# Attention step loop: biases as 128x32 matmuls beside the products, and a new order of the matmuls of a step

## The reference

```
proj = x @ w_in.T                     # k, v, q, 16 heads of 8 columns
bias[h, i, j] = f_h(i - j)            # a sum of 16 Gaussians of the distance
logits = q @ k.T / sqrt(8) + bias
out = softmax(logits) @ v
```

## Time and profile before

| | |
|---|---|
| median of three runs | 1123.06 us (1118.01 to 1123.2) |
| span of the profiled execution | 1119.0 us (its time outside the span is not shown) |
| granted TensorE clock, mean over the span | 0.931 |
| PE busy | 975.8 us, 87% of the span |
| DVE busy | 853.2 us, 76% |
| ACT busy | 677.5 us, 61% |
| POOL busy | 487.5 us, 44% |
| attention's step loop | about 70 to 503 us |

### The profile page before, as it was taken

The page is one execution under the profiler, slowest core; times in us unless marked ns, Lnnn a source line. Parts: engine busy times, 40 slices in busy tenths (PEclk is TensorE's granted clock), DMA queues, the critical chain, the costliest instruction groups (busy, mean ns, idle before and its releaser), DMA issues. The chain is left out here.

```text
span 1119.0 us, 17095 instructions
## 1 busy us (share of the span) xinstructions
PE 975.8 (87%) x5565; PEld 543.6 (49%) x5565; DVE 853.2 (76%) x2203; ACT 677.5 (61%) x1042; POOL 487.5 (44%) x454
## 2 busy tenths in 40 slices
PE   4889999999999999994999999972777449999998
PEld 2413232223222322323777888731566337778886
DVE  7688888889888988766798555477897787975543
ACT  4226656565656565562668888768334126788886
POOL 4400101101110110101788999814674027889997
PEclk9559999999999999996999999987899659999999
DMA  4930224131313230003466677300000035676973
GB/s 100 281 107 9 79 71 85 35 101 55 71 34 104 53 70 2 1 2 87 143 177 175 160 198 191 96 20 1 0 0 0 3 93 151 172 179 158 218 197 96
DMA packets 80086, 105.65 MB, mean 94 GB/s; under 512 B 17741, under 2 KB 41091, under 8 KB 80003
## 3 DMA queue, kind: packets, MB, share of 16 engines
q1 hardware_dynamic: 78119, 102.42, 35.7%
q10 hardware_dynamic: 1883, 2.21, 0.7%
HBM read 95.84 MB, written 8.52 MB: 93 GB/s over the span
## 5 line engine op out<-in xcount | busy, mean ns | idle before, releaser
L663 POOL TENSOR_TENSOR f_act_low<-f_act,f_act_high 128x512 fp32r<-128x512 f32 x272 | 353.0, 1315 | 151.2 <-ACT f_act_high L639 143.5
L1506 DVE CUSTOM_DVE_ANT_0 at_rows<-at_rows,at_table_max 128x512 f32<-128x512 f32 x512 | 340.0, 718 | 43.6 <-PE at_rows L1292 42.9
L1452 ACT ACTIVATE at_prob<-at_cols 128x1024 f32<-128x1024 f32 x256 | 248.2, 1021 | 185.8 <-PE at_cols L1326 185.8
L678 DVE SCALAR_TENSOR_TENSOR f_gated<-f_hid,f_cw 128x512 f32<-128x512 f32 x256 | 174.0, 687 | 115.1 <-ACT f_act L644 86.9
L644 ACT ACTIVATE f_act<-f_gated 128x512 f32<-128x512 f32 x272 | 171.7, 631 | 110.2 <-DVE f_gated L678 78.5
L639 ACT CAST f_act_high<-f_act 128x512 fp32r<-128x512 f32 x272 | 164.7, 606 | 0.0
L1326 PE MATMUL at_cols<-at_table_cols,flip_sum 128*64 128x512 f16 x1024 | 139.3, 389 | 0.0
L1338 PE MATMUL at_pv<-at_prob,at_v_stack 128*32 128x512 f32 x1024 | 137.2, 608 | 0.2 <-ACT at_prob L1452 0.2
L1292 PE MATMUL at_rows<-at_k_stack,at_q_stack 48*128 48x512 bf16 x512 | 122.5, 408 | 12.8 <-DVE at_maxima L1506 10.1
L610 PE MATMUL f_acc<-f_act_high,wd_high 128*128 128x512 f32 x272 | 109.4, 402 | 9.0 <-POOL f_act_low L663 8.8
L1292 PEld LDWEIGHTS at_rows<-at_k_stack,at_q_stack 48*128 48x128 bf16 x512 | 28.9, 93 | 170.2 <-DVE at_maxima L1506 116.8
(11 more groups left out here) (322 smaller groups left out, 1351.0 us busy)
## 6 DMA issues: line engine op xcount, KB each, us to landing
f_cw<-f_c_rows SPq DMA_DIRECT2D x256, 256.0 KB, 4.5
at_table_cols<-bias_rows SPq DMA_DIRECT2D x32, 248.0 KB, 5.1
at_table_max<-bias_rows SPq DMA_DIRECT2D x12, 480.0 KB, 4.6
at_q_stack<-q_parts SPq DMA_DIRECT2D x32, 96.0 KB, 2.5
at_k_stack<-k_parts SPq DMA_DIRECT2D x24, 96.0 KB, 3.8
at_raw_weights<-in_L_ffn_up_w_dram SPq DMA_DIRECT2D x8, 256.0 KB, 4.3
at_raw_weights<-in_L_ffn_down_w_dram SPq DMA_DIRECT2D x8, 256.0 KB, 4.9
at_table_max<-bias_rows ACTq DMA_DIRECT2D x4, 480.0 KB, 8.0
```

Of the source, the lines that this page charges most:

```text
L663: nc.gpsimd.tensor_tensor(act_l[:, n % PART_SLOTS, :], act[:, n % ACT_SLOTS, :], act_h[:, n % PART_SLOTS, :].bitcast(F32), ALU.subtract).t ...
L678: ins = nc.vector.scalar_tensor_tensor(out=gated[:, n % GATE_SLOTS, :], in0=hid[:, n % HID_SLOTS, :], scalar=0.0, in1=cw[:, k % C_SLOTS, u ...
L1452: act(prob[:, S % 2, 2 * hp:2 * hp + 2, :], s2[:, hp, :, :], ACT.Exp).then_inc(exp_done, 1)
L1506: nc.vector.tensor_tensor_reduce(out=slot, in0=slot, in1=t_max[:, 2 * p.hp + j, c:c + BANK][:, ::-1], scale=1.0, scalar=-3.0e38, op0=ALU.a ...
```

## The change

Biases are made with sixteen matmuls of 32 output columns instead of eight of 64 in a step, each with half the columns of `flip_sum`, on four column strips as the products have them. And all steps have one order: first pair, scores 0, turned maxima (where there are any), second pair, scores 1, the wait for the bias table (where a chunk of it is new), biases 0 and 1, products of the step before. The slots, their order, DVE's, ACT's, POOL's and SP's programs stay as they are.

```diff
                 def biases(S, hp):
                     for j in range(2):
-                        for u in range(2):
-                            c = step_columns(S % STEPS, u)
-                            last = mm(s2[u * HALF:(u + 1) * HALF, hp, j, :], m.flip_sum[:],
+                        for w in range(4):
+                            c, k0 = step_columns(S % STEPS, w // 2), 32 * (w % 2)
+                            last = mm(s2[32 * w:32 * (w + 1), hp, j, :], m.flip_sum[:, k0:k0 + 32],
                                       t_col[:, 2 * hp + j, c:c + BANK], start=False, stop=True)
                     last.then_inc(cols_ready, 1)
...
-                    if pairs:
-                        for hp in range(2):
-                            scores(S, hp)
-                        if phase_turned_in(S) is not None:
-                            turn_maxima(phase_turned_in(S))
-                        if it % BATCH == 0:
-                            for c in range(CHUNKS):
-                                if chunk_starts[c] == s:
-                                    pe.wait_ge(tab_in[c], 32 * (it // BATCH + 1))
-                        for hp in range(2):
-                            biases(S, hp)
-                        for n in pairs[1:]:
-                            rows_pair(n)
-                    else:
-                        for hp in range(2):
-                            scores(S, hp)
-                            biases(S, hp)
-                            if hp == 0 and phase_turned_in(S) is not None:
-                                turn_maxima(phase_turned_in(S))
+                    scores(S, 0)
+                    if phase_turned_in(S) is not None:
+                        turn_maxima(phase_turned_in(S))
+                    for n in pairs[1:]:
+                        rows_pair(n)
+                    scores(S, 1)
+                    if it % BATCH == 0:
+                        for c in range(CHUNKS):
+                            if chunk_starts[c] == s:
+                                pe.wait_ge(tab_in[c], 32 * (it // BATCH + 1))
+                    for hp in range(2):
+                        biases(S, hp)
                     if S > 0:
                         products(S - 1)
```

## The result

After: 1195.92 us (median of four runs, 1192.46 to 1200.12) against 1121.36 for before in the same comparison. The ratio is 1.0694, 95% interval 1.066 to 1.0728: 75 us slower, 1202 was forecast, with a range of 1170 to 1220.

The account below looks back on a forecast made before the run. PE was taken to bound the ordinary step at 3.06 us, with ACT's and DVE's loops close; 74 + 2 + 1 + 2 = +79 on the median 1123.06 gave 1202 us, range 1170 to 1220.

Parts of the forecast that it names:

- The second rows pair waits until 1.23 after the first rows matmul: Ordinary step: PE waits for DVE to free the first of three slots; step 3.66 us against 3.06, +0.60.
- DVE idle about 1 us ahead of each step: Sign the forecast is right: DVE stands idle about 1 us per step ahead of the first rows pair.
- Biases in narrow tiles cost nothing: Bias group of each step: sixteen narrow matmuls again make four waves with the same streaming; nothing added.
- The unknown +12 us: Biases to products: the step from fp16 to fp32 taken as 0, at most 0.10 x 117 = +12 us.
- Special steps: In each phase of eight steps: step 5 +0.24, step 6 +0.65, output step +0.52 us; phase 31.7 against 26.41.
- Steps without rows: Eleven steps without rows: scores 1 waits for the last exp, 3.06 against 2.74 us; +2 us in all.
- ACT's loop: Each step: exp 1.94 us, then 1.12 from its end to the next exp pair, 3.06 around, equal to PE's sum.
- The rival with two changes of shape fewer: Each step: two changes of tile shape instead of four, saving 0.20 x 117 = 23 us; time 1100; chance 4%.
- The clock rival: Step loop: stalls keep PE at 1.2 GHz, near 1480 us; a few drops only, 1215 to 1240; chance 8%.
- steps 2 to 113: Fourteen phases of eight steps in the step loop, each +5.3 us: +74 us.
- steps 114 to 116: Steps after the fourteen phases: +0.6 us each and one 0.5, +2 us in all.
- steps 0 and 1: First steps of the loop, at clock 0.50, where PE's longer waves hide more: +0.4 us each, +1 in all.

Follow-up runs that it names:

- wide_new_order: After's order of the step with before's biases, eight matmuls of 64 columns: 1212.76 us, 1.0841 of before.
- narrow_old_order: Before's order of the step with after's biases, sixteen matmuls of 32 columns: 1114.89 us, 0.9979 of before; run once more, 1117.38 us.
- pair_last: After, with scores 1 moved ahead of the second rows pair: 1172.62 us, 1.0501 of before.
- pool_maxima: Before's order with narrow biases, four of six small maxima instructions moved from DVE to GpSimd: 1110.75 us, 0.9942 of before; run once more, 1109.74 us.

## Why the prediction was right, point by point

- *The second rows pair waits until 1.23 after the first rows matmul, and the step is 3.66.* Shown: 1.24 and 3.61. The 0.05 is products to next rows, 0.96 rather than the 1.00 of rows 2, and a slightly shorter gap from biases to products (0.87 from the first bias wave against 0.90 in the sum): products' weights are now loaded ahead, at 225.73, while the biases still run, where the tile shape stays; in wide_new_order, with a change of shape, only with the products themselves, at 230.90.
- *DVE idle about 1 us ahead of each step.* 0.91.
- *Biases in narrow tiles cost nothing, nor does the step from fp16 to fp32.* Shown by narrow_old_order and by the 0.87 from the first bias wave to the products (225.07 to 225.94): three gaps of 0.22 between the four waves leave 0.21 for the step to the products. The unknown +12 us did not come.
- *Special steps.* Step 5's last rows matmul goes at 1.50 (0.26 late, forecast 0.24), step 6's at 1.89 (0.65 late, as forecast), the output step's at 1.74 (0.50, forecast 0.52). All three stand in the rows of PE below: step 5 with its first rows matmul at 211.55, step 6 at 215.42, an output step at 231.53.

```profile
211.55 0.39 PE L1292 MATMUL at_rows<-at_k_stack,at_q_stack 48*128 48x512 bf16 x2
...
213.05 0.39 PE L1292 MATMUL at_rows<-at_k_stack,at_q_stack 48*128 48x512 bf16 x1 [0.68 <-DVE at_maxima L1499]
...
215.42 0.39 PE L1292 MATMUL at_rows<-at_k_stack,at_q_stack 48*128 48x512 bf16 x2
...
217.31 0.39 PE L1292 MATMUL at_rows<-at_k_stack,at_q_stack 48*128 48x512 bf16 x1 [0.26 <-DVE at_maxima L1499]
...
231.53 0.39 PE L1292 MATMUL at_rows<-at_k_stack,at_q_stack 48*128 48x512 bf16 x2
...
233.26 0.39 PE L1292 MATMUL at_rows<-at_k_stack,at_q_stack 48*128 48x512 bf16 x1 [0.61 <-DVE at_maxima L1499]
```

- *Steps without rows run at ACT's loop, 3.06.* They run at 2.98 against 2.74: scores 1 waits for exp.

```profile
559.85 0.39 PE L1319 MATMUL at_cols<-at_q_stack,at_k_stack 51*128 51x512 bf16 x2
560.68 0.39 PE L1319 MATMUL at_cols<-at_q_stack,at_k_stack 51*128 51x512 bf16 x2 [0.43 <-ACT at_prob L1445]
...
562.84 0.39 PE L1319 MATMUL at_cols<-at_q_stack,at_k_stack 51*128 51x512 bf16 x2
```

  The 3.06 was read from the earlier trace rows, where PE's own sum, not ACT's loop, set the interval; the loop by itself is 0.08 shorter. So before's ACT loop was a little less close than the prediction said.
- *The rival with two changes of shape fewer* was rightly set aside, twice over: the slot wait comes first, and behind it ACT's loop leaves 0.08 of the 0.25 that PE's sum then saves. The Trainium skill (TensorEngine Tiling (Array Packing), Tiling Modes) says that a change of mode drains the engine. The rows agree that a change costs: wide_new_order pays 0.15 a step for one more of them. But a change saved on an engine that then waits is not time saved.
- *The clock rival* came true in small. The clock stayed at 1.00 in ordinary phases, but fell for a step or two in five output steps, at steps 34, 58, 82, 106 and 114: the stretches at 0.72 and 0.81 above hold two. In an output step PE does an us of small matmuls and then waits twice for DVE. Each fall costs about 1.6 (5.53 + 3.83 for two steps that otherwise take 4.11 + 3.61), 8 us in all, which nearly makes up for the ordinary step's 0.05 x 117 = 6 and for the 3 us of the stall near 330 that did not come again. So the sum, 79 for 75, is partly luck: three terms of 3 to 8 us were missed with both signs. By parts of the loop, from scores to scores: steps 2 to 113 hold 71.3 (forecast 74), steps 114 to 116 3.8 (forecast 2, with two falls of the clock in it), the steps without rows 1.6 (forecast 2), and steps 0 and 1 took 1.4 less, where 1 more was forecast.

## What to carry to other kernels

A ring of three buffers with a round trip of 1.23 us lets four fills through only if they are spread: before moving producers together to save switches of an engine, count fills against buffers and ask when the buffer of the first is free again. The saved switches are worth only what the next loop behind leaves of them (here 0.08 of 0.25 us), so work out all loops of a step, not the one that binds. And where an in-order engine must wait in any case, put as much other ready work ahead of the wait as there is (pair_last, 23 us better than after).

## What the runs showed of the hardware that was not expected

- Weights of the products (fp32, 32 columns) are loaded ahead during the biases (fp16, 32 columns) when the shape is the same, and the step loses 0.15 to 0.16 us rather than 0.10 when it is not.
- The granted clock fell from its 2.4 GHz level in output steps of after, where the second pair's two rows matmuls start 0.99 us apart, with PE idle for 0.61 of it, after an us of small ones; the row of the stretch from 200 to 206 has 0.72. It did so in only five of the fourteen output steps, in ten in wide_new_order and in four in pair_last. In before, with fewer waits in those steps, it did not. What picks the steps is not shown.
- A layer that no experiment touched took between 139.9 and 149.2 us at granted clocks of 0.84 to 0.88. Part of that is the run (narrow_old_order alone took 140.1 and 142.8), but both runs of pool_maxima, 147.3 and 149.2, lie above all the others measured.
